# Turning h by DMA, f16 dot products and squares inside the counting: one change to a graph kernel

## What is computed

```python
h = jnp.maximum(_layernorm(x, axis=-1), 0.0)
HW = h @ W
s = HW @ a[:OUT_F, 0]
t = HW @ a[OUT_F:, 0]
e = jax.nn.leaky_relu(s[row] + t[col], negative_slope=ALPHA)
m = jax.ops.segment_max(e, row, num_segments=N_NODES)
ex = jnp.exp(e - m[row])
den = jax.ops.segment_sum(ex, row, num_segments=N_NODES)
att = ex / den[row]
agg = jax.ops.segment_sum(att[:, None] * h[col], row, num_segments=N_NODES)
basis = _b_splines(agg, grid)
out = jax.nn.silu(agg) @ base_w.T + jnp.einsum('nip,oip->no', basis, spline_w)
```

## Time and profile before

| | us |
|---|---|
| median of 3 runs | 613.38 |
| lowest and highest | 612.81, 620.52 |
| the profiled execution | 613.95 |
| its span | 611.8 |
| PE, DVE, ACT, POOL busy in it | 578.0, 435.9, 332.7, 42.9 |

### The profile page before, as it was taken

One profiled execution on the slowest core, in us unless ns is written; L12 is line 12 of the kernel. 1 busy time (PEld: TensorE's weight loads), 2 busy tenths in 40 slices (PEclk: granted clock), 3 DMA queues, 4 the chain that ended last, 5 costly groups with the idle time before them and its releaser, 6 DMA issues.

```text
span 611.8 us, 9451 instructions
## 1 busy us (share of the span) xinstructions
PE 578.0 (94%) x3797; PEld 379.8 (62%) x3797; DVE 435.9 (71%) x717; ACT 332.7 (54%) x420; POOL 42.9 (7%) x40
## 2 busy tenths in 40 slices
PE   4998949999989999999999999999999999999994
PEld 2766848889645555555555555687557855587552
DVE  7999699997679999993499779362474335542555
ACT  4568466569999989891898234044132333142112
POOL 1056100000000000000000030042000020000000
PEclk9999779999998999999999999999999999999998
DMA  9960078662600000000000001240200000000112
GB/s 306 356 239 2 3 180 186 142 90 50 237 1 0 2 2 0 1 1 0 1 2 1 1 1 43 91 193 0 70 1 0 1 1 2 1 0 1 41 43 84
DMA packets 40459, 36.36 MB, mean 59 GB/s; under 512 B 28414, under 2 KB 30078, under 8 KB 40288
## 3 DMA queue, kind: packets, MB, share of 16 engines
q1 hardware_dynamic: 40416, 35.76, 19.5%
HBM read 23.36 MB, written 5.84 MB: 48 GB/s over the span
## 4 chain that ended last, share of the span: by engine, by line
PE 80%; DVE 13%; ACT 2%; issue 2%; DMA 1%; DVEq 1%; ACTq 0%
PE bank L1689 36%; PE bank L1774 21%; PE bank L1731 13%; PE bank L1647 2%; DVE MSK L1140 2%; DVE EX L1153 2%; PE bank L1569 2%; DVE HL L1169 2%; DVE EX L1157 1%; PE bank L1652 1%; DVE OR L1013 1%; DVE BHL L1239 1%; PE bank L1558 1%; PE bank L1524 1%; DMA AT<-HL 1%
## 5 line engine op out<-in xcount | busy, mean ns | idle before, releaser
L1689 PE MATMUL bank<-BHL,WKh 128*128 128x418 f16 x1152 | 206.4, 341 | 2.1 <-DVE BHL L1239 2.1
L1689 PEld LDWEIGHTS bank<-BHL,WKh 128*128 128x128 f16 x1152 | 111.7, 97 | 96.2 <-DVE BHL L1239 2.5
L1774 PE MATMUL bank<-C,YH 128*128 128x418 f16 x360 | 122.4, 340 | 0.0
L1774 PE MATMUL bank<-C,YL 128*128 128x418 f16 x360 | 122.3, 340 | 0.0
L1470 DVE SCALAR_TENSOR_TENSOR Z<-bank,yback,dvb 128x418 f32<-128x418 f32 x36 | 23.4, 651 | 52.1 <-PE bank L1774 52.1
L950 ACT ACTIVATE bnc<-bnm,tiny 128x1 f32<-128x1 f32 x12 | 3.5, 296 | 91.7 <-DVE bnm L1478 91.7
L1774 PEld LDWEIGHTS bank<-C,YH 128*128 128x128 f16 x360 | 35.3, 98 | 28.8 <-issue 0.8
L1647 PE MATMUL bank<-AT,hH 128*128 128x256 f16 (+1 forms) x200 | 45.8, 277 | 7.7 <-DMA AT<-HL 7.7
L1774 PEld LDWEIGHTS bank<-C,YL 128*128 128x128 f16 x360 | 35.2, 98 | 28.0
L912 ACT ACTIVATE YH<-bank,dvl 128x512 f16<-128x512 f32 x30 | 20.4, 686 | 56.6 <-PE bank L1731 56.6
L1416 DVE SCALAR_TENSOR_TENSOR YL<-bank,dvl,YH 128x512 f16<-128x512 f32 x30 | 22.0, 749 | 39.1 <-ACT YH L912 39.1
(11 more groups left out here) (220 smaller groups left out, 963.7 us busy)
## 6 DMA issues: line engine op xcount, KB each, us to landing
WKf<-in_wk SPq DMA_DIRECT2D x9, 1024.0 KB, 6.6
c_scratch<-C SPq DMA_DIRECT2D x10, 320.0 KB, 3.0
C<-c_scratch SPq DMA_DIRECT2D x1, 3200.0 KB, 10.3
GWf<-in_gwT SPq DMA_DIRECT2D x3, 1024.0 KB, 11.5
XT<-in_xT SPq DMA_DIRECT2D x1, 2500.0 KB, 9.3
outT<-Z SPq DMA_DIRECT2D x3, 625.0 KB, 3.0
hx<-in_x SPq DMA_DIRECT2D x1, 1280.0 KB, 6.9
Wt<-in_WT SPq DMA_DIRECT2D x1, 1024.0 KB, 9.1
```

What stands on the lines that cost most here:

```text
L1689: ins = mm(bank[:, 4 * (g % 2) + o, 0:G], lhs, rhs, start=(u == 0 and q == 0 and i == 0), stop=(u == UNITS - 1 and q == PAIR - 1 and i == 2))
L1774: ins = mm(bank[:, u % YB, 0:G], Y[:, j, o * P:(o + 1) * P], C16[:, j, g * G:(g + 1) * G], start=(j == 0 and i == 0), stop=(j == NT - 1 an ...
```

## The change

- h's halves are turned by DMA: SP issues, behind its loads, 20 transposes (10 tiles, high and low half) of 128 x 512 f16 into a new `hT` for all 10 tiles.
- ACT rounds the tile right behind its relu (`rounded`), DVE subtracts (`low_half`, one group later); POOL has no part in it. `H_AT` replaces `TURN_AT`.
- PE's transposes, f32 dot products and spreads go. In their place stand f16 products: `rows` (12 matmuls, one for each of three sets of tiles, straight into `trow`) and `cols` (8 matmuls of 2 columns for each tile), with the vectors divided by their norm and split into f16 halves (`bounds`, now 8 instructions on DVE). The exponential multiplies the norm back.
- The 144 matmuls of the squares stand behind the counts of groups 8 to 16, 16 in each; DVE reads the diagonal behind group 17, and `weight_scale` moves from attention step 6 to step 4.
- `source_columns`, three small DVE instructions, stands between `largest(0)` and `bent_row(0)`.
- The copies of `C16` to HBM start one attention step later.

```diff
-TURN_AT = (5, 6, 8, 9, 11, 12, 14, 15, 16, 17)
+H_AT = (5, 6, 7, 8, 9, 11, 12, 13, 14, 15)
+ROWS_IN = (11, 16, 18)
+COLS_IN = (12, 17, 18)
+H_SETS = ((0, 4), (4, 8), (8, 10))
+SQUARES_AT = 8
 # SP, behind the loads
+            sp.wait_ge(wa_done, 1)
+            for b, (t0, t1) in enumerate(H_SETS):
+                for t in range(t0, t1):
+                    sp.wait_ge(h_high, t + 1)
+                    sp.dma_start(hT[:, 0, :, t * P:(t + 1) * P], hH[:, t, :], transpose=True).then_inc(hT_in[b], 16)
+                    sp.wait_ge(h_low, t + 1)
+                    sp.dma_start(hT[:, 1, :, t * P:(t + 1) * P], hL[:, t, :], transpose=True).then_inc(hT_in[b], 16)
...
-                for t in range(2 * s, min(2 * s + 2, NT)):
+                for t in range(2 * s - 2, 2 * s) if 1 <= s <= NT // 2 else ():
 # POOL
-            for t in range(NT):
-                pool.wait_ge(h_high, t + 1)
-                nc.gpsimd.tensor_tensor(hL[:, t, :], hx[:, t, :], hH[:, t, :], ALU.subtract).then_inc(h_low, 1)
 # ACT
+            def rounded(t):
+                act.wait_ge(h_rows, t + 1)
+                nc.scalar.copy(hH[:, t, :], hx[:, t, :]).then_inc(h_high, 1)
...
             def rows_low(b):
                 c0, c1 = b * 512, min((b + 1) * 512, NP)
-                act.wait_ge(st_done, c1 // P)
+                act.wait_ge(rows_in, b + 1)
+                if b == 2:
+                    act.wait_ge(cols_in, len(H_SETS))
...
                 for t in range(NT):
-                    if n == TURN_AT[t]:
-                        turned(t)
-                for t in range(NT):
-                    if n == TURN_AT[t] + 1:
-                        dots(t)
-                for t in range(NT):
-                    if n == TURN_AT[t] - 1:
+                    if n == H_AT[t]:
                         activations(t)
+                        rounded(t)
 # DVE
+            def low_half(t):
+                dve.wait_ge(h_high, t + 1)
+                V.tensor_tensor(hL[:, t, :], hx[:, t, :], hH[:, t, :], ALU.subtract).then_inc(h_low, 1)
...
                 for t in range(NT):
-                    if n == TURN_AT[t] + ROUND_AT:
-                        rounded(t)
+                    if n == H_AT[t] + 1:
+                        low_half(t)
+                if n == SQUARES_AT + SQUARE_BLOCKS:
+                    block_squares()
+                    dve.wait_ge(sq_read, 1)
+                    V.tensor_copy(wsc[:, 0:1], wss[:, 0:1]).then_inc(sumsq_set, 1)
 # PE
+            def rows(b):
+                t0, t1 = H_SETS[b]
+                pe.wait_ge(hT_in[b], 32 * (t1 - t0))
+                pe.wait_ge(wn_set, 1)
                 for c in range(DC):
+                    for i, k in ((0, 0), (1, 0), (0, 1)):
+                        ins = mm(trow[:, t0 * P:t1 * P], down(wsplit[:, i, c, 1:2]), hT[:, k, c, t0 * P:t1 * P],
+                                 start=(c == 0 and i + k == 0), stop=(c == DC - 1 and k == 1))
+                ins.then_inc(rows_in, 1)
...
             for n in range(GROUPS):
                 pe.wait_ge(onehots, n + 1)
                 if n >= 2:
                     pe.wait_ge(sub_copied, n - 1)
                 count(n)
...
+                if SQUARES_AT <= n < SQUARES_AT + SQUARE_BLOCKS:
+                    block_squares(n - SQUARES_AT)
+                for b in range(len(H_SETS)):
+                    if n == ROWS_IN[b]:
+                        pe.wait_ge(ctl_set, 1)
+                        rows(b)
+                    if n == COLS_IN[b] and b == 2:
+                        pe.wait_ge(sumsq_set, 1)
+                        mm(bank[:, 2, SUM_AT:SUM_AT + 1], ones[:, :], wsc[:, 0:1], start=True, stop=True).then_inc(sumsq_done, 1)
+                    if n == COLS_IN[b]:
+                        cols(b)
```

More of the change, by code:

```diff
@@ L314, in build @@
         bound_set = sem("bound_set")
[L315 to L319, removed]
+        hT_in = [sem(f"hT_in{b}") for b in range(len(H_SETS))]
+        wn_set = sem("wn_set")
+        rows_in = sem("rows_in")
+        cols_in = sem("cols_in")
+        sbend_set = sem("sbend_set")
         st_set = sem("st_set")
@@ L716, in _ @@
                         rows_low(b)
+            rows_low(2)
             columns_out()
-            rows_low(2)
             def exponential(s):
@@ L1152, in bent_row @@
                 dve.wait_ge(masked, s + 1)
-                V.scalar_tensor_tensor(ex(s), trow, st[:, s, 2:3], LOW[:, :], ALU.add, ALU.max).then_inc(bent, 1)
+                V.scalar_tensor_tensor(ex(s), trow, sbend[:, s:s + 1], LOW[:, :], ALU.add, ALU.max).then_inc(bent, 1)
             def attention(s):
@@ L1255, in copied, with source_columns @@
                 ins.then_inc(kan_copied, 1)
-            V.tensor_scalar(near[:, :], st[:, :, 3:4].rearrange("p t k -> p (t k)"), bnd[:, 0:1], None, ALU.add)
+            def source_columns():
+                dve.wait_ge(st_set, 1)
+                V.tensor_tensor(sbend[:, :], st[:, :, 0:1].rearrange("p t k -> p (t k)"),
+                                st[:, :, 1:2].rearrange("p t k -> p (t k)"), ALU.add)
+                dve.drain()
+                V.tensor_scalar(sbend[:, :], sbend[:, :], BEND, None, ALU.mult)
+                dve.drain()
+                V.tensor_scalar(near[:, :], sbend[:, :], SHIFT, bnd[:, 2:3], ALU.subtract, ALU.mult).then_inc(sbend_set, 1)
+                dve.wait_ge(sbend_set, 1)
             for s in range(2):
                 largest(s)
+                if s == 0:
+                    source_columns()
                 bent_row(s)
@@ L1580, in _, with cols @@
+            def cols(b):
+                for t in range(*H_SETS[b]):
+                    for c in range(DC):
+                        for k in range(2):
+                            ins = mm(bank[:, 2, ST_AT + 2 * t:ST_AT + 2 * t + 2], hT[:, k, c, t * P:(t + 1) * P],
+                                     wsplit[:, 0:2 + k:1 + k, c, 0], start=(c == 0 and k == 0),
+                                     stop=(c == DC - 1 and k == 1))
+                ins.then_inc(cols_in, 1)
             for n in range(GROUPS):
```

147 lines of the change are left out of this document (50 added, 97 removed).

## The result

| | before | after |
|---|---|---|
| median (4 runs each) | 613.84 | 624.87 |
| lowest and highest | 612.81, 620.52 | 624.57, 627.29 |
| the profiled execution, its span | 613.95, 611.8 | 624.59, 622.8 |
| first masked maximum starts | 66.98 | 76.57 |
| spline layer starts (its first product in PE's timeline) | 155.98 | 166.85 |

The ratio is 1.0165, with a 95% interval of 1.0088 to 1.0241: 5 to 15 us slower, 11 by the medians. Nearly all of it arises ahead of the spline layer (10.9 of the 11.0 us by which the spans differ): 9.6 in the counting, 1.3 in attention. The earlier trace rows has the spline layer of the kernel before at 156.14, since the chain of waits cuts the product ahead of it otherwise than the timeline; the two traces are compared by the timeline here.

What follows compares the result with a forecast made beforehand. Bound: the counting's waits, mostly on PE, other engines close behind. Counting 5.0 later, `source_columns` 0.6, diagonal -0.3, clock 0.8: 613.95 + 6.1 = 620.05 for the profiled execution, 619.5 us as median; range 613.5 to 628.5.

Steps and rivals of the forecast that it cites:

- the main term: Counting stage: DVE's first masked maximum was to start at 72.0 instead of 66.98, 5.0 us later.
- The walk: Counting followed group by group over DVE, PE and ACT from one-hots 6 to the first masked maximum at 72.0.
- I take 0.74, since the bytes are what both share: Transposes of h: 0.74 us each at 512 columns, price going with size; eight take 5.9 us.
- The start at 41.5: First transpose on SP's queue, behind the spline weights and `gpar`, was to start at 41.5 us.
- The lower level was given 0.8: `rows(0)` on PE at the lower clock would add 2.6 us; a third, 0.8, was counted.
- 5.0 + 0.8: Counting: 5.0 us later first masked maximum by the walk, plus 0.8 for `rows(0)` perhaps at the lower clock.
- The loop decides: Counting: one-hots, count, copy, relu, rounding, with DVE waiting for the rounding; 4.8 us for two groups, against DVE's own 2.1 each.
- a sign against it: DVE's subtractions in the counting: each was to wait about 0.3 to 1 us; finding tiles ready would make the prediction wrong.
- The other sign: PE's products in the counting running at the lower level behind 55 us would make the prediction wrong.
- With transposes that cost nothing the walk still gives 617: Counting, within the faster rival (607 us, chance 0.12): free transposes alone give only part, 617 us.
- Attention was to keep its length within 0.5: From first masked maximum to spline layer: 89.2 us as before, within 0.5.
- same price at any width, at 1.3 us each 624: Rival on transposes: cost independent of width, at 1.3 us each 4.4 more, 624; chance 0.10 for over 1.1 each.

Runs made afterwards that it cites:

- e1: Changed kernel with two tiles a transpose, 10 of 128 x 1024 in place of 20 of 128 x 512: 622.83 us, ratio 1.0137 to the kernel before.
- e2: Changed kernel with `rows(0)` behind group 13 instead of 11, `cols(0)` and `rows_low(0)` behind 14: 621.25 us, ratio 1.0102 to the kernel before.
- e5: Changed kernel with only the high halves transposed, ten transposes instead of twenty, low halves left out of the scores: 618.79 us, ratio 1.0067 to the kernel before.
- e8: Changed kernel with four tiles a transpose, six transposes (2048 columns, the last set 1024): 621.25 us, ratio 1.0129 to the kernel before.
- e3: Changed kernel with every DVE subtraction two groups behind its relu and rounding instead of one: 622.25 us, ratio 1.0122 to the kernel before.
- e9: Changed kernel with only the high halves transposed and every subtraction one group later: 615.89 us, ratio 1.0016 to the kernel before.
- e10: Changed kernel with 28 unused products of 128 columns on PE ahead of its wait for the first transposes: 625.85 us, ratio 1.0159 to the kernel before.
- e7: Changed kernel with a program constant for the factor in the exponential and bias steps, instead of a memory operand: 622.98 us, ratio 1.0170 to the kernel before.
- e4: Changed kernel with the squares, DVE's diagonal and the sum moved back into attention: 624.37 us, ratio 1.0166 to the kernel before.
- e11: Changed kernel with e8's transposes, sets at groups 12, 17, 18, subtractions of tiles 0 to 7 one group later, squares back in attention: 621.76 us, ratio 1.0087.
- e12: As e11, with the first set in four transposes of 1024 columns: 622.28 us, ratio 1.0154 to the kernel before.
- e6: Changed kernel with the first set's transposes issued ahead of the last spline weights on SP's queue: 622.48 us, ratio 1.0155 to the kernel before.

## Why the prediction held within its range, and missed by five, step by step

The time lies in the range (613.5 to 628.5), 5.4 us over the forecast of 619.5. That it lies in it is in part luck, since two errors of the main term went against each other.

- **The walk was right to 0.7 us up to the one-hots of group 10.** One-hots 6 were forecast at 28.9 and stood at 29.1; 7 at 32.6 (32.7); tile 1 rounded at 33.6 (33.9); one-hots 8 at 35.8 (36.2); tile 3 rounded at 40.3 (40.9); one-hots 10 at 42.5 (43.2). `bounds` took 26.45 to 27.49, the 1.0 forecast. OM was 0.41 to 0.48 everywhere. PE was done with group 11 at 47.9 instead of 46.5, since its squares took 1.87 and not 0.9; the wait for DMA covered that.
- **The step that was mis-sized is the transpose, "I take 0.74, since the bytes are what both share".** For the engines that was near (0.64), but at 512 columns it is the queue that sets the pace, 1.31 us an issue. Eight cost 11.35 instead of 5.9, 5.4 more. The start at 41.5 was wrong the other way, by 3.05: `gpar` took 6.9 us to land, and the first transpose was issued 0.6 behind it. So `rows(0)` began at 38.45 + 11.35 + 1.37 = 51.17 instead of 41.5 + 5.9 + 1.5 = 48.9. With the start as forecast it would have been 54.2, and the time near 628 by an estimate from these rows. e1 shows that the price hardly goes with the width, e2 that the queue is never free, e5 what half the issues give: 5.3 us.
- **The lower level was given 0.8 and took 1.8 at `rows(0)` alone** (4.44 instead of 2.6), 0.8 in the squares of group 16 and 0.5 at `rows(1)`. `rows(0)` took 2.75 in e5 and e8, where PE had stood for 0.46 and 1.06 us, and 4.16 to 5.28 in the change and ten runs, where it had stood for 1.55 to 8.43. In e2, e3, e9 and e10 the squares ahead of the wait still took 1.08: there the level fell over the wait. In the change they took 1.87, so the level was down before the wait, and what part of the 1.8 the wait caused is not shown; e8's `rows(1)` took 4.60 with no wait just before it. That filling the gap would win it back is argued, not shown (e10). The forecast's sentence that PE was at the lower level up to 43 us before rests on lengths alone; the granted clock of 38 to 42 us reads 1.00.
- **From the end of `rows(0)` on the walk held**: to the first maximum 21.0 us, forecast 20.4 (19.5 to 21.0 in three profiles of this order). Of the 3.8 over the forecast 5.0 + 0.8, some 2.3 are the later start of `rows(0)`, 1.0 its length and 0.6 what lies behind it.
- **"The loop decides" was half right.** Its waits of DVE are there, on tiles 1, 3, 5 and 8, and the chain of waits goes through them; but tiles 0, 2, 4, 7 and 9 were ready, which the forecast had named as a sign against it. No gain from taking the waits out shows while the queue lies behind (e3); 2 us or more shows when it does not (e9 against e5). The other sign that came in part is the lower level behind 55 us, in group 16 and `rows(1)`.
- **"With transposes that cost nothing the walk still gives 617"**, 3.6 over before: e5, where they cost PE 0.46, is 2.1 to 6.1 over.
- **Attention was to keep its length within 0.5; it took 90.3 us where it had 89.0, both by the timeline.** `source_columns` cost 0.64 as forecast: from the first maximum to the first bent row 2.18 us, before 1.54 (start of L1140 in the earlier trace rows and of L1153 at 68.52). Missed was the operand from memory, 1.8 (e7), a term put at nothing. Without it the stretch is 88.5, so the rest of the change gave back some 1.2 instead of 0.3: 0.5 by squares and diagonal (e4), the other 0.7 not traced to one edit.
- **A cost of the squares in the counting is not shown** (e4).
- **The rival "same price at any width, at 1.3 us each 624" came out at 624.87**, but not by its sum: its 4.4 for eight transposes were 2.3 by the earlier start, and clock and operand made up the rest. It had 0.10 for a price of over 1.1. The trace of before already spoke for it, in two rows of SP's queue from the stretch that the forecast took its 1.84 from:

```profile
124.92 1.33 SPq L522 DMA_TRANSPOSE AT<-HL  x1
128.44 1.25 SPq L524 DMA_TRANSPOSE AT<-HL  x1
```

AT's issues hold the queue for 1.25 to 1.35 us here. The forecast read what the engines need and not what the queue needs; whether an issue of 512 columns would be cheaper no row of before says.

## What to carry to other kernels

A transfer has two prices, what its issue takes on the queue and what its bytes take on the engines. Read both from the trace and take the dearer one. Here the issue of a transpose was the dearer at 512 columns, and a row of a wider one in the trace of before already gave it; joining transfers can pay only until the bytes are as dear. Where the work of several engines is moved onto one queue, ask when its last item is issued, and what stands behind the first engine that waits for it: one wait of PE stopped ACT and DVE as well. An edit that shows no gain alone may be the next bound; try it again with the first one out of the way. And before a microsecond is put down to an edit, compare two profiles of the same code.

## What was not expected of the hardware

- An issue of a DMA transpose takes SP's queue 1.26 us at 512 columns and 1.23 to 1.34 at 1024, as AT's at 1280 (median 1.34). At 2048 it takes 1.4 to 3.7, and pairs of them 4.4 to 5.6 (e8, e11, e12). Single issues were held longer: 2.0 to 2.6 at 512 columns, 2.2 to 4.3 at 1024.
- Amid loads of 1 MB each the landing of a 512 wide transpose takes 6.6 us at the median, behind them 2.5 (e6 and the change).
- A factor read from memory adds 92 ns to an exponential of 1280 columns, and 60 to a DVE step of one column.
- TensorE's level differs between executions at the same work: the 16 squares of group 9 took 1.08 in one (e7) and 1.87 in others. What decides it there stays open.
